# Starting the first feed-forward chunk of a macaron block before the second chunk's transposes

## The reference

```python
x = x + 0.5 * _L0_ffn_ref(_layernorm(x), ...)   # mixture of experts: top 2 of 8, 4 MLPs and 4 KANs
x = x + _L0_attn_ref(_layernorm(x), ...)        # attention and a gated feed-forward
x = x + 0.5 * _L0_ffn_ref(_layernorm(x), ...)   # the same mixture of experts again
```

```python
h = n + attention(layernorm(n, ln1_g, ln1_b), wq, wk, wv, wo)
out = h + silu(z @ w1) * (z @ w3) @ w2          # z = layernorm(h, ln2_g, ln2_b); w1, w3: 128 x 352; w2: 352 x 128
```

## Time and profile before

| | us |
|---|---|
| median of three runs | 675.87 |
| the profiled execution | 682.9 |
| its span in the trace | 681.1 |
| the block of the change, first matmul to the next block's first work | 394.97 to 449.25 |

### The profile page before, as it was taken

One profiled execution on the slowest core, in us unless ns is written; L12 is line 12 of the kernel. 1 busy time (PEld: TensorE's weight loads), 2 busy tenths in 40 slices (PEclk: granted clock), 3 DMA queues, 4 the chain that ended last, 5 costly groups with the idle time before them and its releaser, 6 DMA issues. The chain is left out here.

```text
span 681.1 us, 18347 instructions
## 1 busy us (share of the span) xinstructions
PE 541.0 (79%) x6060; PEld 470.9 (69%) x6061; DVE 450.8 (66%) x1166; ACT 373.6 (55%) x876; POOL 264.3 (39%) x305
## 2 busy tenths in 40 slices
PE   5347899999997277886999939972489899999960
PEld 4237899999986234664788834672378899999960
DVE  5743778787877496998133384458438688787855
ACT  2335888888944026500555612223358798888930
POOL 6035466666544246700000020120354566666530
PEclk9999999999999779767899978965589999999985
DMA  8972222100100400000000000059610000101106
GB/s 240 370 282 73 64 71 69 31 27 27 28 15 16 132 1 3 2 13 1 16 4 4 5 0 1 0 169 342 268 36 21 27 27 31 31 27 27 24 16 189
DMA packets 41235, 46.51 MB, mean 68 GB/s; under 512 B 7216, under 2 KB 33184, under 8 KB 40160
## 3 DMA queue, kind: packets, MB, share of 16 engines
q1 hardware_dynamic: 32224, 34.00, 15.2%
q0 software_dynamic: 4736, 9.71, 5.2%
q10 hardware_dynamic: 4224, 2.10, 1.0%
HBM read 35.69 MB, written 10.09 MB: 67 GB/s over the span
## 5 line engine op out<-in xcount | busy, mean ns | idle before, releaser
L845 PE MATMUL k_y_ps<-kan_w,k_basis 128*128 x1056 | 127.3, 280 | 8.2 <-DVE k_basis L941 5.7
L845 PEld LDWEIGHTS k_y_ps<-kan_w,k_basis 128*128 128x128 f32 x1056 | 123.9, 196 | 9.9 <-issue 9.8
L835 PE MATMUL k_z_ps<-kan_w,k_basis 128*128 x528 | 119.9, 380 | 1.9 <-issue 1.9
L1107 ACT ACTIVATE k_sig<-k_h1T 128x256 f32<-128x256 f32 x264 | 84.5, 402 | 53.0 <-DVE k_h1T L966 45.3
L835 PEld LDWEIGHTS k_z_ps<-kan_w,k_basis 128*128 128x128 f32 x528 | 97.7, 190 | 14.6 <-issue 2.3
L941 DVE SCALAR_TENSOR_TENSOR k_basis<-k_sig 128x512 f32<-128x512 f32 x132 | 85.8, 691 | 15.7 <-ACT k_sig L1107 13.9
L1100 ACT ACTIVATE k_sig<-k_h0T 128x128 f32<-128x128 f32 x280 | 59.2, 294 | 6.6 <-DVE k_h0T L929 6.6
L1670 ACT ACTIVATE got<-p_ps 128x960 f32<-128x960 f32 (+1 forms) x44 | 39.2, 944 | 27.6 <-PE p_ps L1586 27.6
L661 POOL DMA_INDIRECT y_rows<-k_y,k_rows x33 | 33.2, 1005 | 50.2 <-DVE k_y L973 32.3
L1634 DVE TENSOR_REDUCE p_minus_max<-p_ps 128x6 f32<-128x960 f32 (+1 forms) x44 | 46.2, 1119 | 6.5 <-PE p_ps L1551 5.1
L813 PE MATMUL m_z_ps<-m_xT,m_w 128*128 128x128 f32 x304 | 45.0, 296 | 5.4 <-DVE m_z L989 2.5
(11 more groups left out here) (252 smaller groups left out, 1039.8 us busy)
## 6 DMA issues: line engine op xcount, KB each, us to landing
kan_w<-in_L_ffn_kan_sl_W_dram SPq DMA_DIRECT2D x16, 1024.0 KB, 10.0
x_rows<-got SPq DMA_DIRECT2D x4, 1024.0 KB, 12.4
mlp_w<-in_L_ffn_mlp_W_dram SPq DMA_DIRECT2D x2, 1024.0 KB, 5.8
mlp_w<-in_L_ffn_mlp_W_dram SPq DMA_DIRECT2D x8, 256.0 KB, 6.7
got<-y_rows SPq DMA_DIRECT2D x8, 256.0 KB, 4.9
got<-y_rows ACTq DMA_DIRECT2D x8, 256.0 KB, 5.6
xs<-in_L_attn_x_dram SPq DMA_DIRECT2D x4, 256.0 KB, 3.6
s_cos<-in_cos_dram SPq DMA_DIRECT2D x8, 128.0 KB
```

The source lines that it names most:

```text
L835: last = nc.tensor.matmul(z_ps, basis0[:, g], k.kan_w0[:, bass.ds(e, 1), g], start=(g == 0), stop=(g == G - 1))
L845: last = nc.tensor.matmul(y_ps, basis1[:, g, c], k.kan_w1[:, bass.ds(e, 1), c, g], start=(g == 0 and c == 0), stop=(g == G - 1 and c == F2 ...
L1107: ins = nc.scalar.activation(sig1[:, g], h1T[:], ACT.Sigmoid, bias=float(-GRID[g]))
```

## The change

PE no longer waits with the feed-forward of chunk 0 until chunk 1 is transposed. Behind the turn of chunk 0 it does parts 0 and 1 of chunk 0, then the turn of chunk 1, and then part 2 of chunk 0. Part 2 can't go with the other two without a wait, because it writes the buffers of part 0. ACT follows the same order: `affine(0)`, silu of parts 0 and 1, `affine(1)`, silu of part 2. DVE does the gates of parts 0 and 1 of chunk 0 right behind `normalize(1)`, ahead of `normalize(2)`. From chunk 1 on the order is the old one, and no instruction is added or removed.

```diff
-                def by_w1_w3(g):
+                def by_w1_w3(g, parts=range(3)):
                     pe.wait_ge(nT_ready, g + 1)
-                    for c, (at, size) in enumerate(HIDC):
+                    for c in parts:
+                        at, size = HIDC[c]
                         v = 3 * g + c
                         if v >= 2:
                             pe.wait_ge(hid_ready, v - 1)
...
                 turn_n2(0)
-                for g in range(NCH):
+                by_w1_w3(0, range(2))
+                turn_n2(1)
+                by_w1_w3(0, range(2, 3))
+                for g in range(1, NCH):
                     if g + 1 < NCH:
                         turn_n2(g + 1)
                     by_w1_w3(g)
-                    if g:
-                        by_w2(g - 1)
+                    by_w2(g - 1)
                 by_w2(NCH - 1)
...
+                def silu(g, c):
+                    size = HIDC[c][1]
+                    act.wait_ge(u_done, 3 * g + c + 1)
+                    if g:
+                        act.wait_ge(hid_ready, 3 * g + c - 2)
+                    nc.scalar.activation(gate[0:size, c], u1_ps[(3 * g + c) % 2][0:size],
+                                         ACT.Silu).then_inc(silu_done, 1)
+
                 affine(0)
-                for g in range(NCH):
+                silu(0, 0)
+                silu(0, 1)
+                affine(1)
+                silu(0, 2)
+                for g in range(1, NCH):
                     if g + 1 < NCH:
                         affine(g + 1)
-                    for c, (at, size) in enumerate(HIDC):
...
+                    for c in range(3):
+                        silu(g, c)
...
                 normalize(1)
+
+                def gated(g, c):
+                    size = HIDC[c][1]
+                    dve.wait_ge(silu_done, 3 * g + c + 1)
+                    if g >= 2:
+                        dve.wait_ge(y_done, g - 1)
+                    nc.vector.tensor_tensor(hid[g % 2][0:size, c], gate[0:size, c], u3_ps[(3 * g + c) % 2][0:size],
+                                            ALU.mult).then_inc(hid_ready, 1)
+
+                gated(0, 0)
+                gated(0, 1)
                 dve.wait_ge(h_added, NCH)
...
                 for g in range(NCH):
                     if g + 2 < NCH:
                         normalize(g + 2)
-                    for c, (at, size) in enumerate(HIDC):
...
+                    for c in range(3):
+                        if g or c == 2:
+                            gated(g, c)
                     if g:
                         add_ffn(g - 1)
```

More of the change, by code:

```diff
@@ L1797, in _ @@
                 act.preload_act_table(ACT.Silu)
-                affine(0)
-                for g in range(NCH):
+                def silu(g, c):
[5 more added lines that the diff above has]
+                                         ACT.Silu).then_inc(silu_done, 1)
+                affine(0)
+                silu(0, 0)
[3 more added lines that the diff above has]
+                for g in range(1, NCH):
                     if g + 1 < NCH:
                         affine(g + 1)
-                    for c, (at, size) in enumerate(HIDC):
[L1803 to L1807, removed]
+                    for c in range(3):
+                        silu(g, c)
             @block.gpsimd
```

## The result

The changed kernel took 674.25 us (median of 20 runs, 671.0 to 677.33); the kernel before took 677.37 in 20 runs (675.6 to 682.89). The ratio of the two is 0.9927, with a 95% interval of 0.9909 to 0.9944: 0.73% faster, about 4.9 us. The two medians themselves lie 3.1 us apart and the two means 4.3, so the size of the gain in the total is known to about 1 us only. The forecast was 5.15 us, or 0.76%.

The account below looks back on a forecast made before the run. PE's hole until DVE normalized chunk 1, then PE's work alone, bounded the block. Removing 3.44 and 2.6 us against 0.4 and 0.5 added gave about 5.1; 5.15 step by step, so 675.87 became 670.7 us, range 667 to 676.5.

Parts of the forecast that it names:

- The sum: Up to chunk 1's start: 3.44 us of parts and 2.6 of half-clock loss go, 0.4 and 0.5 come back: 5.1.
- the case without a fall: At part 0: PE's clock stays at full, PE waits for DVE alone, chunk 1 starts at 413.05, gain 5.7 us.
- the smaller gain: Total of 671.5 to 676 us: clock late in the new place, or runs at the spread's upper end; chance 18%.
- The clock, the term whose size was off: At parts 0 and 1 on PE: half clock from 405.4, full clock back after 3.3 us, at 408.7.
- the other end: At parts 0 and 1: PE's clock needs 5.2 us to return, until 410.6.
- The lower end of the gain: With 5.2 us for the clock's return, chunk 1 starts at 414.5, a gain of 4.25 us.
- The start of part 0: On PE behind `affine(0)`: input there at 405.14, a weight load of 0.34 us first, start at about 405.4.
- The new wait ahead of the third turn: Ahead of chunk 2's turn: PE waits for `normalize(2)`, queued behind part 1's gate, about 0.5 us.
- The signs of being wrong: Clock at 0.50 past 411; part 2 waits for a gate; third-turn stall over 1.5 us; later stretch changes over 2 us.
- The slower rival: In the block: PE's clock doesn't come back because of short bursts with pauses; total 686.6 us; chance 4%.
- The larger gain: In the next block: the clock holds through PE's pause, an estimated 3.5 us more, total 667.2 us; chance 15%.

Follow-up runs that it names:

- the first profile: The one profiled execution of the changed kernel without further edits, against the kernel before; span 671.8 us, block 48.2 us instead of 52.2.
- the control: The changed kernel with the four expert-loop counts loaded with asserted bounds; 0.9958 of the kernel before, block 46.8 us.
- the two controls: The kernel before and the changed kernel, each with asserted bounds on the four expert-loop counts; 1.0016 and 0.9958 of the kernel before.
- the clock alone: The kernel before's order with asserted counts, plus idle matmuls keeping PE working in its pauses; 0.9964 of the kernel before, block 49.6 us.
- the clock held up: The changed kernel with asserted counts, plus idle matmuls ahead of and behind the turn of chunk 0; 0.993 of the kernel before, block 46.4 us.
- one part: The changed kernel with asserted counts, but only part 0 ahead of the turn of chunk 1; 0.9961 of the kernel before, block 47.9 us.
- the late residual: The changed kernel with asserted counts and chunk 3's residual moved later on DVE, behind the gate of part 1; 0.9944 of the kernel before.
- the order of PE and ACT alone: The changed kernel with asserted counts, but DVE keeping its old order, gates of parts 0 and 1 behind `normalize(2)`; 0.9949 of the kernel before.

## Why the prediction was right

- **What bounds the block, and what the change removes.** Confirmed: PE's hole was time in which ready work could be done, parts 0 and 1 fill it, and what follows is a plain shift (30.5 us from chunk 1 to the next block in both profiles).
- **The sum.** Forecast 5.15 us; the block gained 4.0 in the first profile and 5.4 in the control's, and once more 5.4 with the idle matmuls behind the block, where the order up to there is the same. In the total it is 0.73%, about 4.9 us, in the first 20 runs, and 0.58%, about 4.0, between the two controls. The two causes were told apart: 2.6 us for the clock alone (forecast 2.6), and 3.2 for the order with the clock held up (forecast 3.1, the 5.7 of the case without a fall less 2.6). With the clock up, chunk 1 came at 15.9, and the sum's end for that case is 16.0; the sum had PE wait for `normalize(2)` there, and what held it was `normalize(1)`, then part 2, which ended 0.3 us after `normalize(2)`. That the two numbers meet to 0.1 us is in part luck.
- **The median.** 670.7 was forecast and 674.25 measured, 3.55 us more. 1.5 us of it is the base: 20 runs of before have their median at 677.37, three had it at 675.87. The other 2.05 are a difference of medians of 3.1 us instead of 5.15; how much of them is a clock that came back late and how much scatter isn't shown. The median lies in the band of the smaller gain (671.5 to 676, 18%), and its two causes, a late clock and the upper end of the spread, are the ones at work. The range held because it took them in.
- **The clock, the term whose size was off.** I took 3.3 us for its return and 5.2 as the other end. In the first profile it took 5.9, in the control 3.1. The argument for 3.3 was that PE starts just behind the fall; that is borne out by five profiles (0.3 to 0.5 us behind it, back in 2.9 to 3.1) and not by the first (0.9 behind it, back in 5.9). The lower end of the gain, 4.25, was too high by 0.25.
- **The start of part 0.** I had put a weight load of 0.34 us at the half clock ahead of it, 405.4. PE started 0.05 behind `affine(0)`, which is 405.2 in those times; the term was 0.2 too large.
- **The new wait ahead of the third turn.** Forecast 0.5 us; 0.29 in the first profile. Its cause was right, since moving `normalize(2)` removed it.
- **The signs of being wrong.** Three of the four were met, by little. The clock stayed at 0.50 until 14.1 us behind DVE's first add, which is 411.1 in the prediction's times (sign: 411). Part 2 waited about 0.1 us for the gate of part 0 in the control. The stretch behind the block was 2.4 us shorter (sign: 2), which is the scatter of that stretch in all profiles here. None touches the mechanism: the signs were set tighter than the clock and the scatter allow.
- **The slower rival.** It didn't come: behind the return of the clock PE stood at 1.00 until the end of the block in every profile here, through waits of 0.3 to 1.5 us. The Trainium skill's page "TensorE: Matmul & The Clock Gate", section "A second HAM failure mode: psum-queue depth-cycling", reports a kernel whose clock kept switching through such brief pauses. This case's traces don't agree behind chunk 0's parts; ahead of them, among the smaller matmuls of `by_wo` and the first turn, the clock did switch, up at 398.26 and down again at 405.08.
- **The larger gain.** Given 15% for a clock that holds by luck. In eleven profiles it never did. It takes a cause; with one, 2.7 of the forecast 3.5 us arrive.

## What to carry to other kernels

A hole on TensorE can cost more than the work that could have filled it: behind the hole of 5.79 us here the next matmuls ran at half the clock, 2.6 us on top of 3.4. So look for work whose inputs are ready at the start of the hole, and count the half clock into its price, at either end of what the trace shows for its return. One profile is one draw of the moment at which the clock changes; measure such a stretch from a fixed event and in more than one profile before you explain a difference of 1 or 2 us. And where removing one limit brings almost nothing, look for a second that ends at the same moment before you call the first one harmless.

## What the runs showed of the hardware

- The granted clock fell while PE was not yet idle for long. In the profile after, it fell at 401.38, as the four transposes ended that had started at 400.73 behind 1.82 us of idle. In the nine profiles without idle matmuls in this block, PE's order is the same up to there, and the fall came between 6.0 and 8.0 us behind DVE's first add: ahead of the four transposes in one, at their end in another and behind them in seven. So it can't be read from the length of the last pause alone.
- Where PE started part 0 0.3 to 0.5 us behind the fall, the full clock was back in 2.9 to 3.1 us (five profiles: the control of the change, one part, `normalize(2)` between the gates, the late residual, and the idle matmuls behind the block); where it started 0.9 behind, in 5.9, and 2.6 behind, in 4.2 (the order of PE and ACT alone). Before the change it was 5.0 behind, and 5.2. The start of the block shows the same: of the thirteen profiles, eight have `by_wo` start 0.1 to 0.5 us behind a fall, with the clock back in 2.9 to 3.3 us, and the profile after, again 0.9 behind, has it back in 5.9; in the other four the clock fell 0.6 to 1.2 us after `by_wo` had started and was back 4.0 to 4.6 us after that start.
- Idle matmuls into a buffer that nobody reads cost about 0.1 us or nothing where PE waits anyway (the turn of chunk 0 at 6.71 behind DVE's first add instead of 6.60). Six of them ahead of the second turn, in the order of before, were worth 2.6 us. Four behind the block brought the first matmul of the experts to 35.7 us in one profile and to 38.0 in the other, against 38.2 to 39.0 without them.
- A gather by indices, issued while the DMA engines were busy for all of the time (a share of 1.03 from 450 to 475 with the idle matmuls behind the block), was 5.8 us on the way to its matmul (470.96 to 476.75), and between 5.4 and 6.3 in all thirteen profiles. The DMA engines were still busy for all of 478 to 479 (1.00), so it didn't wait for the weights' transfers to end.
